# The last graph's 32-wide layer in the room of the first two layers, and new drain sequences

## The reference, cut to what matters

```python
x = layernorm(x + L0(x, adj))   # A: attention, 4 heads of 64, masked by adj
x = layernorm(x + L1(x, adj))   # G: gated graph layer, 4 heads of 256, tanh scores
x = layernorm(x + L2(x, adj))   # B: 8 heads of 32; here is what it computes:
    m      = x @ map_w.T + map_b
    n      = m per head / max(norm, 1e-8);  cos = n n^T
    scores = q k^T / sqrt(32), masked where adj is set;  p = softmax(scores)
    a      = (cos > 0.1) * p                      # the "cut"
    out    = relu(a @ (x @ gcn_map_w.T + b) @ gcn_W.T / (sum(a) + 1))
x = layernorm(x + L3(x, adj))   # D: attention, as A with other weights
```

## Time and profile before

| | |
|---|---|
| median of three runs | 2638.91 us |
| profiled execution: span | 2634.6 us |
| outside the span, against the median | 4.3 us |
| busy in the span | TensorE 2561.4 us (97%), VectorE 2006.3 (76%), ScalarE 1409.9 (54%), POOL 917.0 (35%) |
| mean granted TensorE clock | 0.989 |

### The profile page before, as it was taken

One profiled execution on the slowest core, in us unless ns is written; L12 is line 12 of the kernel. 1 busy time (PEld: TensorE's weight loads), 2 busy tenths in 40 slices (PEclk: granted clock), 3 DMA queues, 4 the chain that ended last, 5 costly groups with the idle time before them and its releaser, 6 DMA issues.

```text
span 2634.6 us, 63306 instructions
## 1 busy us (share of the span) xinstructions
PE 2561.4 (97%) x22097; PEld 2293.3 (87%) x22097; DVE 2006.3 (76%) x6629; ACT 1409.9 (54%) x3925; POOL 917.0 (35%) x988
## 2 busy tenths in 40 slices
PE   7999999999999999999999999999999999999985
PEld 7888888898888899888889888889888889888874
DVE  3577877777877787877887787787787787787764
ACT  2355555655654555555565555565565555565442
POOL 3233333343333344333334333334333334433330
PEclk9999999999999999999999999999999999999997
DMA  4000000000000000000000000000000000000000
GB/s 135 7 1 12 11 11 0 10 10 10 10 10 9 1 10 10 10 10 9 1 10 10 10 10 10 0 10 10 10 10 10 4 6 10 10 10 0 11 6 9
DMA packets 44490, 29.90 MB, mean 11 GB/s; under 512 B 21264, under 2 KB 44048, under 8 KB 44432
## 3 DMA queue, kind: packets, MB, share of 16 engines
q1 hardware_dynamic: 44432, 29.13, 3.8%
HBM read 20.73 MB, written 8.39 MB: 11 GB/s over the span
## 4 chain that ended last, share of the span: by engine, by line
PE 84%; ACT 5%; DVE 2%; issue 1%; POOL 0%; ACTq 0%; DVEq 0%; POOLq 0%
PE bank L462 21%; PE bank L464 19%; PE bank L463 19%; PE bank L1420 4%; ACT arena L594 4%; PE bank L519 4%; PE bank L528 3%; PE bank L451 3%; PE bank L1411 3%; PE bank L539 3%; PE bank L1402 2%; PE bank L1430 2%; DVE arena L678 1%; PE bank L1244 1%; DVE b L635 0%
## 5 line engine op out<-in xcount | busy, mean ns | idle before, releaser
L393 POOL TENSOR_SCALAR l_ve<-l_mv 128x2 f32<-128x2 f32 x128 | 28.8, 225 | 1022.2 <-DVE l_mv L378 1021.9
L1571 ACT ACTIVATE b<-b,s_sh 128x256 f32<-128x256 f32 x512 | 254.8, 503 | 97.4 <-DVE s_sh L635 97.4
L462 PE MATMUL bank<-arena_r 128*128 128x256 f32 x1024 | 303.1, 296 | 0.2
L464 PE MATMUL bank<-arena_r 128*128 128x256 f32 x1024 | 289.1, 282 | 0.0
L463 PE MATMUL bank<-arena_r 128*128 128x256 f32 x1024 | 289.0, 282 | 0.0
L1836 POOL TENSOR_TENSOR arena_r<-a,arena_r 128x512 fp32r<-128x512 f32 x128 | 165.5, 1293 | 335.8 <-ACT arena_r L1508 335.7
L1831 POOL TENSOR_TENSOR arena_r<-a,arena_r 128x512 fp32r<-128x512 f32 x128 | 166.7, 1303 | 165.9 <-ACT arena_r L1514 165.9
L1733 DVE SCALAR_TENSOR_TENSOR b<-bank,b 128x256 f32<-128x256 f32 x512 | 191.0, 420 | 36.0 <-ACT b L1571 27.6
L462 PEld LDWEIGHTS bank<-arena_r 128*128 128x128 f32 x1024 | 194.7, 190 | 21.4 <-issue 21.2
L635 DVE CUSTOM_DVE_ANT_0 b<-bank,s_add 128x256 f32<-128x256 f32 x512 | 181.5, 420 | 23.9 <-PE bank L1402 14.8
L463 PEld LDWEIGHTS bank<-arena_r 128*128 128x128 f32 x1024 | 195.2, 191 | 0.0
(11 more groups left out here) (280 smaller groups left out, 9041.7 us busy)
## 6 DMA issues: line engine op xcount, KB each, us to landing
x_in<-in_x SPq DMA_DIRECT2D x32, 256.0 KB, 2.8
out<-x SPq DMA_DIRECT2D x32, 256.0 KB, 2.1
adj_a<-in_adj SPq DMA_DIRECT2D x32, 64.0 KB, 2.5
adj_b<-in_adj SPq DMA_DIRECT2D x32, 64.0 KB, 1.8
a<-in_L_gnn_W SPq DMA_DIRECT2D x4, 256.0 KB, 3.3
b<-in_L_gnn_A_w SPq DMA_DIRECT2D x1, 1024.0 KB, 7.6
arena<-in_L_gnn_attn SPq DMA_DIRECT2D x4, 256.0 KB, 7.2
g_b_wh<-in_L_gnn_bW SPq DMA_DIRECT2D x1, 512.0 KB, 9.2
```

Source lines behind the costliest of these rows:

```text
L462: pe.matmul(out, w[0], x[0], start=first, stop=False)
L464: return pe.matmul(out, w[1], x[0], start=False, stop=last)
L1571: last = act.activation(S.e[:, n, it, :], S.e[:, n, it, :], ACT.Exp, bias=S.sh[:, it, h:h + 1], scale=-1.0, accum_out=S.sums[:, it, h:h + 1])
```

## The change

A class `Room` names the banks and SBUF places that B works in. `S.home` is what B had: banks `BB`, places of `b32`, the same banks and places for both quads. `S.wide` is used for the last graph only (`is_last`): banks `BA` for the head of the layer and the first quad, `BB` for the second quad; SBUF places 0 to 6 and 12 of the arena for the head, 8 to 11 and 4 to 7 for the first quad, 13 to 16 and 17 to 20 for the second.

With it B(31) no longer waits for D(30) in `b_x_t`, `b_m`, `b_k` and `b_sem`, and its second quad no longer for its first; `b_scores(31, 1)` waits for four signals of D(30) instead. `masked` and `copy_t` lose waits in the same way. All other graphs keep their banks, places and waits.

The four `DRAIN` lists are written anew, with the same steps in another order. `FILL` and `ORDER` are unchanged.

```diff
+class Room:
+    def __init__(self, banks, late_banks, sem, qt, kt, ut, m, sq, u, ot, e, at):
+        self.banks, self.quad_banks = banks, (banks, late_banks)
...
+def is_last(g):
+    return isinstance(g, int) and g == GRAPHS - 1
...
+        S.home = Room(BB, BB, b32(0), b32(1), b32(2), b32(3), b32(4), b32(5), b32(6), b32(12),
+                      (b32(8, 4), b32(8, 4)), (b32(4, 4), b32(4, 4)))
+        S.wide = Room(BA, BB, plain(0), plain(1), plain(2), plain(3), plain(4), plain(5), plain(6), plain(12),
+                      (plain(8, 4), plain(13, 4)), (plain(4, 4), plain(17, 4)))
...
             def b_x_t(g):
+                R = b_room(g)
                 pe.wait_ge(G.norm.out.sem, G.norm.out.at(g))
-                if later(g):
+                if later(g) and not is_last(g):
                     pe.wait_ge(D.p_t_act.sem, D.p_t_act.all(g - 1))
-                pe_transpose_rows(pe, BB[2], x2, C.ident).then_inc(S.x_t_psum.sem, 1)
+                pe_transpose_rows(pe, R.banks[2], x2, C.ident).then_inc(S.x_t_psum.sem, 1)
...
             def b_scores(g, q):
...
+                elif is_last(g):
+                    pe.wait_ge(D.p_t_act.sem, D.p_t_act.all(g - 1))
+                    pe.wait_ge(D.p_t_dve.sem, D.p_t_dve.all(g - 1))
+                    pe.wait_ge(D.o_sb.sem, D.o_sb.all(g - 1))
+                    pe.wait_ge(D.norm.sum.sem, D.norm.sum.all(g - 1))
                 else:
                     pe.wait_ge(S.a_t_act.sem, S.a_t_act.at(g, 2 * q))
...
             def masked(g, h):
-                if h >= QUAD:
+                if h >= QUAD and not is_last(g):
                     dve.wait_ge(S.a_t_psum.sem, S.a_t_psum.at(g, h - QUAD + 1))
```

More of the change, by code:

```diff
@@ L220 @@
[L220 to L224, removed]
@@ L225 @@
-        ("d_scores_0", 0), ("d_scores_1", 0), ("d_probs_0", 0), ("d_probs_1", 0), ("d_probs_2", 0), ("d_probs_3", 0),
-        ("d_values_0", 0), ("d_values_1", 0), ("d_out", 0),
+        ("d_q", 2), ("d_k", 2), ("d_v", 2), ("d_scores_0", 2), ("d_scores_1", 2), ("a_q", 0), ("a_k", 0),
[3 rows of a table added]
+        ("b_m", 1), ("b_q", 1), ("b_sem", 1), ("g_x_t", 0), ("g_adj_t", 0), ("b_k", 1), ("g_c", 0), ("g_z_0", 0),
[6 rows of a table added]
+        ("b_out", 1), ("g_ha_2_1", 0), ("g_ha_3_1", 0), ("g_ha_3_0", 0), ("g_ha_t", 0), ("g_gate_x", 0), ("d_x_t", 1),
@@ L251 @@
-        ("b_copy_4", 1), ("g_p_3", 0), ("b_relu_1", 1), ("g_ha", 0), ("g_ha_t", 0), ("d_x_t", 1), ("g_gate", 0),
-        ("d_q", 1), ("d_k", 1), ("d_exps_0", 1), ("d_exps_1", 1), ("d_exps_2", 1), ("d_exps_3", 1), ("d_probs_0", 1),
-        ("d_probs_2", 1), ("d_o_copy", 1), ("b_x_t", 0), ("b_q", 0), ("b_k", 0), ("b_unit_t", 0), ("b_exps_0", 0),
[3 rows of a table removed]
[1 row of a table added]
+        ("b_q", 1), ("g_x_t", 0), ("g_c", 0), ("g_z_0", 0), ("b_k", 1), ("b_unit_t", 1), ("g_z_1", 0), ("g_wh_0", 0),
[4 rows of a table added]
+        ("b_copy_6", 1), ("g_p_3", 0), ("b_relu_1", 1), ("g_ha", 0), ("g_ha_t", 0), ("d_x_t", 1), ("g_gate", 0),
@@ L257 @@
+        ("d_k", 1), ("d_q", 1), ("b_x_t", 0), ("d_exps_0", 1), ("d_exps_1", 1), ("d_exps_2", 1), ("d_exps_3", 1),
+        ("b_k", 0), ("d_probs_0", 1), ("d_probs_2", 1), ("d_o_copy", 1), ("b_q", 0), ("b_unit_t", 0), ("b_exps_0", 0),
[3 rows of a table added]
         ("d_exps_3", 0), ("d_probs_0", 0), ("d_probs_2", 0), ("d_o_copy", 0),
@@ L290 @@
[L290 to L293 removed]
[4 rows of a table removed]
[L298 removed]
+        ("b_sem", 2), ("g_adj_t", 1), ("g_wh_0", 1), ("b_unit", 2), ("g_z_0", 1), ("d_stats", 3), ("g_wh_1", 1),
[5 rows of a table added]
@@ new lines @@
+        ("b_copy_5", 2), ("g_p_3", 1), ("b_scale", 2), ("b_sum", 2), ("b_stats", 2), ("g_diff", 1), ("b_norm_out", 2),
+        ("g_ha_t", 1), ("d_x_t", 2), ("g_gate", 1), ("a_x_t", 0), ("g_mix", 1), ("g_sum", 1), ("g_stats", 1),
[3 rows of a table added]
+        ("a_probs_3", 0), ("d_o_copy", 2), ("b_x_t", 1), ("a_o_copy", 0), ("d_sum", 2), ("d_stats", 2), ("a_sum", 0),
+        ("a_stats", 0), ("b_m", 1), ("a_norm_out", 0), ("b_square", 1), ("g_x_t", 0), ("g_adj_t", 0), ("b_unit", 1),
[6 rows of a table added]
+        ("b_stats", 1), ("b_norm_out", 1), ("g_ha_t", 0), ("g_diff", 0), ("d_x_t", 1), ("g_gate", 0), ("g_mix", 0),
@@ L858, in build, with b_room @@
         norm_buffers(ctx, nc, S.norm, "l2", x3)
-        S.qt, S.kt, S.ut = b32(1), b32(2), b32(3)
-        S.m, S.sq, S.u, S.sem = (b32(n) for n in (4, 5, 6, 0))
         S.xt = split(b32r, 0)
-        S.e, S.at, S.ot = b32(8, 4), b32(4, 4), b32(12)
+        S.home = Room(BB, BB, b32(0), b32(1), b32(2), b32(3), b32(4), b32(5), b32(6), b32(12),
+                      (b32(8, 4), b32(8, 4)), (b32(4, 4), b32(4, 4)))
+        S.wide = Room(BA, BB, plain(0), plain(1), plain(2), plain(3), plain(4), plain(5), plain(6), plain(12),
+                      (plain(8, 4), plain(13, 4)), (plain(4, 4), plain(17, 4)))
+        def b_room(g):
+            return S.wide if is_last(g) else S.home
         S.ss, S.fl, S.inv = (sb(f"s_{n}", [P, T * HS]) for n in ("ss", "fl", "inv"))
@@ L1364, in b_m @@
                 pe.wait_ge(S.x_t_sb.sem, S.x_t_sb.at(g))
-                if later(g):
+                if later(g) and not is_last(g):
                     pe.wait_ge(D.norm.sum.sem, D.norm.sum.all(g - 1))
-                pe_node_major(pe, BB[1], S.xt, S.w_m).then_inc(S.m_psum.sem, 1)
+                pe_node_major(pe, R.banks[1], S.xt, S.w_m).then_inc(S.m_psum.sem, 1)
             def b_q(g):
+                R = b_room(g)
                 pe.wait_ge(S.x_t_sb.sem, S.x_t_sb.at(g))
-                pe_feature_major(pe, BB[2], S.w_q, S.xt).then_inc(S.q_psum.sem, 1)
+                pe_feature_major(pe, R.banks[2], S.w_q, S.xt).then_inc(S.q_psum.sem, 1)
@@ L1373, in b_k @@
             def b_k(g):
+                R = b_room(g)
                 pe.wait_ge(S.x_t_sb.sem, S.x_t_sb.at(g))
-                if later(g):
+                if later(g) and not is_last(g):
                     pe.wait_ge(D.p_t_dve.sem, D.p_t_dve.all(g - 1))
-                pe_feature_major(pe, BB[3], S.w_k, S.xt).then_inc(S.k_psum.sem, 1)
+                pe_feature_major(pe, R.banks[3], S.w_k, S.xt).then_inc(S.k_psum.sem, 1)
             def b_sem(g):
+                R = b_room(g)
                 pe.wait_ge(S.x_t_sb.sem, S.x_t_sb.at(g))
-                if later(g):
+                if later(g) and not is_last(g):
@@ L1401, in b_scores @@
                         rows = slice(DHS * n, DHS * n + DHS)
-                        last = pe.matmul(BB[n][:, it * NODES:(it + 1) * NODES], S.qt[rows, q, it * P:(it + 1) * P],
-                                         S.kt[rows, q, :], start=True, stop=True)
+                        last = pe.matmul(R.quad_banks[q][n][:, it * NODES:(it + 1) * NODES], R.qt[rows, q, it * P:(it + 1) * P],
+                                         R.kt[rows, q, :], start=True, stop=True)
                 last.then_inc(S.s_psum.sem, 1)
             def b_cos(g, q):
+                R = b_room(g)
                 pe.wait_ge(S.max.sem, S.max.at(g, QUAD * q + QUAD))
@@ L1410, in b_cos @@
                         rows = slice(DHS * n, DHS * n + DHS)
-                        last = pe.matmul(BB[n][:, it * NODES:(it + 1) * NODES], S.ut[rows, q, it * P:(it + 1) * P],
-                                         S.ut[rows, q, :], start=True, stop=True)
+                        last = pe.matmul(R.quad_banks[q][n][:, it * NODES:(it + 1) * NODES], R.ut[rows, q, it * P:(it + 1) * P],
+                                         R.ut[rows, q, :], start=True, stop=True)
                 last.then_inc(S.cos_psum.sem, 1)
             def b_transpose(g, h):
+                R = b_room(g)
                 n = h % QUAD
@@ L1717, in masked @@
                 dve.wait_ge(S.s_psum.sem, S.s_psum.at(g, h // QUAD + 1))
-                if h >= QUAD:
+                if h >= QUAD and not is_last(g):
                     dve.wait_ge(S.a_t_psum.sem, S.a_t_psum.at(g, h - QUAD + 1))
-                elif later(g):
+                elif later(g) and not is_last(g):
                     dve.wait_ge(S.a_t_psum.sem, S.a_t_psum.at(g - 1, HS - QUAD + n + 1))
```

123 lines of the change are left out of this document (65 added, 58 removed), and 106 rows, old and new, of the table DRAIN.

## The result

The changed kernel takes 2621.3 us (median of four runs, 2615.6 to 2622.5) against 2638.7 before: ratio 0.9937, interval 0.9925 to 0.9949. The forecast was 2621, range 2616 to 2629. The profiled execution of the changed kernel took 2622.45 us with a span of 2620.5, so 1.9 us lie around the span.

A forecast was written before the change was run, and what follows sets the result against it. The loop was taken as TensorE-bound, with no engine busy throughout in the tail, where B(31) runs alone. Gains 8.9 + 7.6 + 1.2 = 17.7 us give 2616.9 + 4.3 = 2621.2; forecast 2621 us, own range 2617 to 2625, wider range 2616 to 2629.

The forecast's parts named there:

- Start of B(31): Last graph's 32-wide layer: masks start at about 2564.9 instead of 2573.80, 8.9 us gained.
- Both groups open: B(31), eight heads in one run: first mask to last copy 16.1 us instead of 23.7, 7.6 gained.
- High throughout: 14.2, so 1.9 better: B(31), first mask to last copy: with TensorE's clock high throughout, 14.2 us, 1.9 better than forecast.
- The rest of the drain: Stretch 2464 to 2482 behind the loop: 1.2 of TensorE's 2.2 us of waits taken as gained.
- Neighbour on POOL: B(31)'s inverse norms on POOL beside D(30)'s second normalisation: 0.4 us taken; ends 0 and 3.3.
- Around the span: Outside the profiled span of 2634.6: 4.3 us to the median 2638.91, added again to the new span.
- Low clock from b_m on: Rival: TensorE stays at 1.2 GHz from b_m on, costing some 7 us, 2628; chance 0.11.
- Half only: Rival: D(30) with B(31)'s head threaded through runs late, masks start no sooner than 2573.8; 2630, chance 0.09.
- POOL's hold: Rival: A(31)'s and B(30)'s masks delay G(30)'s reciprocal root on POOL; at 37 us of hold 2645; chance 0.05.
- All falling well: Rival: high clock throughout and all 2.2 us of TensorE's waits behind the loop gained, 2618; chance 0.04.
- the third term: The 1.2 us gain expected from TensorE's waits between 2464 and 2482, behind the loop.

The follow-up runs named there:

- kernel with the late start: Changed kernel with both head groups open in the wide room, but B(31)'s instructions up to its first scores behind D(30)'s, as before: 2628.7 us, ratio 0.9968.
- early lists only: Kernel before with the new order lists only up to graph 31's gate in G; afterwards old lists and old room: 2637.9 us, ratio 0.9997.
- masks first: Changed kernel with VectorE masking all eight heads of B(31) before cutting, and ScalarE's eight exponentials ahead of its copies: 2618.0 us, ratio 0.9930.
- the kernel that was to show it: Changed kernel with B(31)'s cosines head by head, written several times, and identity transposes ahead of five stages of D(31): 2641.8 us, ratio 1.0022.
- POOL beside: Changed kernel with POOL's mask of D(31) moved behind B(31)'s inverse norms and one more power, its result unread: 2620.2 us, ratio 0.9939.
- D(31) filled: Changed kernel with only TensorE's waits in D(31) filled with 8 to 40 identity transposes into an unread bank: 2617.2 us, ratio 0.9927.
- late lists only: Changed kernel with the old lists up to graph 31's gate in G, new ones from D(30) on, wide room: 2619.6 us, ratio 0.9931.
- all that helped: Changed kernel with VectorE's masks first in B(31), POOL's D(31) mask behind the inverse norms, TensorE's D(31) waits filled with transposes: 2612.8 us, ratio 0.9909.

## Why the prediction was right, step by step

**Start of B(31): right.** Three marks from the store, predicted and then measured: output of G(31) 206.20 and 206.53; D(30)'s statistics done 223.8 and 223.6; first mask 223.9 and 223.58, that is 8.9 and 9.18 sooner than before. The kernel with the late start, 9.80 behind the changed one, shows that the earlier start causes it. The 0.33 us at the output of G(31) is a neighbour that the prediction had not counted. The new list of POOL puts B(31)'s mask beside G(31)'s mix (the step `g_mix`), a product of two SBUF operands that takes 0.69 us in the kernel before and in early lists only, where that mask runs earlier:

```profile
2546.20 1.02 DVE L1740 SCALAR_TENSOR_TENSOR a<-a 128x512 f32<-128x512 f32 x1 [0.77 <-ACT a L1595]
```

```profile
2546.05 1.51 POOL L1931 TENSOR_SCALAR s_add<-adj_b 128x512 bf16<-128x512 uint8 x1
```

**Both groups open: 7.6 predicted, 7.57 measured, the size by luck in part.** The clock came as taken, low for the transposes of four heads and high for the rest, but its price did not. The first cosines came at the high clock and not "2.09 us as now"; the transposes began 9.05 us behind the first mask (8.6 by the prediction), the first sixteen (four heads) at 1.2 GHz, the rest at the higher. By stage, after:

```profile
2576.47:2579.00 2.53, 2.53 (x16) 2.53 (x13) 2.39 (x13) 0.60 (x1) 0.00 (x0) 0.50 0.00 0
2579.00:2582.50 3.50, 2.80 (x22) 2.32 (x21) 2.60 (x11) 2.55 (x7) 1.34 (x2) 0.95 0.21 75
```

But "High throughout: 14.2, so 1.9 better" put VectorE's 1.9 us of waits down to the clock alone. They are 0.83 + 0.46 + 0.44 = 1.73 us, and the order of VectorE's and ScalarE's instructions removes them at the low clock: with masks first the stretch is 14.54 us at a mean grant of 0.77, and with POOL's mask out of the way 14.16 at 0.76. In the old order the second cosines waited for mask 7 behind two cuts. Whether a high clock in the old order would have removed them too is not shown, as the kernel that was to show it fell to the low one. Nor did the four heads cost 0.92 us each at the low clock, as I took from the earlier trace rows: sixteen transposes took 2.53, 0.63 a head, at the same grant of 0.50; before, the cuts that the transposes need ran beside them, so the 0.92 most likely held waits for these. The 1.9 us of the sum for slow transposes and the 1.73 us of waits that it did not foresee, for the second cosines, for the transposes behind them and for exponential 7, are nearly the same size: that is luck.

**The rest of the drain: wrong, the mis-sized term.** "I take 1.2 us of these 2.2 as gained"; measured 0.29 lost at the first mask (early lists only). Of the 2.2 us of waits 0.63 are left in their place, 0.83 stand elsewhere, and the busy time grew. Without it the sum of the other two, 16.5, stands beside 16.90 between the two traces: 9.18 + 7.57 + 0.15. That the median came within 0.3 us of 2621 although 1.2 us of the sum are not there is luck too: one median against another is known to some 3 us.

**Neighbour on POOL.** 0.4 taken; the four normalisations beside the power took 1.18 us against 1.12 without one, 0.06. The Trainium skill ("SBUF — State Buffer", section "SBUF: two separate sides") has whichever of VectorE and GpSimd takes the shared pair of ports first hold it for the whole instruction, while the other blocks; no row here shows that of VectorE. G(31)'s mix began 0.15 us behind POOL's mask and ended at 2547.22, ahead of the mask's end at 2547.56; it became 0.33 us longer.

**Around the span.** I added 4.3 us, the median less the profiled span. It is 1.9 in the changed kernel's own pair of numbers; if it was as much before, the profiled execution was a short one. The difference to the median was used on both sides, so it did no harm.

**Rivals.** Low clock from b_m on (2628): 0.91 was granted in the stretch. Half only (2630): falls with the first mask. POOL's hold (2645): G(30)'s root does start 3.4 us later behind the store than before, 127.19 against 123.79, behind A(31)'s and B(30)'s masks; but no wait of TensorE between the store and D(30)'s first scores is over 0.84 us, so the hold was covered. All falling well (2618): neither the clock nor the third term did.

## What to carry to other kernels

A gain in a tail is the sum of how much sooner its head starts and how much shorter its chain is; a kernel with each alone measures both, and marks behind one fixed instruction tell tenths of a microsecond where medians spread over several. Idle time in a window of a full engine is a loss only if the work behind the window also comes sooner without it; before two windows are compared, they are shifted to the same mark. A lone last stage at the low clock can be made faster by transposes of the identity in TensorE's idle time, here by 3.5 us with 99 of them over all 128 rows.

## What the runs showed of the hardware that I had not expected

- TensorE, busy 25.00 of 25 us with products over 32 rows, several on end over the same rows, was granted 0.50; in D(31), with its waits filled by transposes over 128 rows, it was granted 0.95. A TensorE that the profile shows as busy throughout can be at 1.2 GHz.
- The same cosines of the first group took 1.15 us in the changed kernel and 2.09 in the kernel with POOL beside, at the same place behind a wait of 2.69 us in both: the granted clock behind one and the same wait differs between executions. Of six kernels with that wait (2.69 or 2.70 us), the changed one, masks first and D(31) filled took 1.15, and late lists only, POOL beside and all that helped took 2.09. The row with POOL beside:

```profile
2567.40 2.09 PE L1441 MATMUL bank<-arena 32*128 32x256 f32 x16 [2.69 <-DVE s_sh L647]
```

- POOL and VectorE stretch each other, but not all of their instructions. With masks first, the output of D(30) (one source, SBUF to SBUF) took 1.11 us beside POOL's mask and 0.74 without; an addition from a bank (0.69) and statistics (0.75) beside the same mask did not change (POOL beside). The two rows with masks first, VectorE's and POOL's:

```profile
2574.24 1.11 DVE L397 TENSOR_SCALAR x<-x,l_mv,l_rs 128x256 f32<-128x256 f32 x2
```

```profile
2574.59 1.94 POOL L733 TENSOR_SCALAR l_add<-adj_b 128x512 bf16<-128x512 uint8 x1
```

- The loop's last store was issued at 2337.67 to 2343.84 us in the twelve profiled executions, with the same instructions ahead of it: a spread of 6 us that arises ahead of the change, more than most single terms here.
